# RWKV attention and a mixture of experts on one core: experts' hidden split ahead of the next rows, slot buffers doubled, V differences on VectorE, new order in the last project round, at the seam and in the first output batch

## The reference, cut to what matters

```python
# attention (RWKV): a token's mix with the token before it, four projections, a scan, one projection out
xx = prev - x;  xk, xv, xr, xg = (x + xx * tm for tm in (tm_k, tm_v, tm_r, tm_g))
r, k, v, g = xr @ Wr.T, xk @ Wk.T, xv @ Wv.T, sigmoid(xg @ Wg.T)
# scan over t, e = exp(k_t): out = (a + exp(u) e v) / (b + exp(u) e);  a = w a + e v;  b = w b + e
attn = layernorm((sigmoid(r) * wkv * g) @ Wo.T) * ln_g + ln_b
# experts: rms norm, 32 experts, each token takes its 4 best, at most 256 tokens an expert
probs = softmax(z @ w_router);  w_topk, sel = top_k(probs, 4)
y[e] = (silu(buf[e] @ w_gate[e]) * (buf[e] @ w_up[e])) @ w_down[e]        # 512 -> 352 -> 512
shared = sigmoid(z @ w_shared_gate) * ((silu(z @ sw_gate) * (z @ sw_up)) @ sw_down)   # 512 -> 1408 -> 512
```

## Time and profile before

| | us |
|---|---|
| median of 3 runs (1730.23 to 1732.56) | 1730.6 |
| the profiled execution, own time | 1733.92 |
| its span, first to last instruction | 1732.0 |
| first expert's first product | 448.35 |
| first product of the output stage | 898.23 |
| PE idle in the engine's rows | 4% |

### The profile page before, as it was taken

One profiled execution on the slowest core, in us unless ns is written; L12 is line 12 of the kernel. 1 busy time (PEld: TensorE's weight loads), 2 busy tenths in 40 slices (PEclk: granted clock), 3 DMA queues, 4 the chain that ended last, 5 costly groups with the idle time before them and its releaser, 6 DMA issues.

```text
span 1732.0 us, 26222 instructions
## 1 busy us (share of the span) xinstructions
PE 1661.9 (96%) x8496; PEld 1403.0 (81%) x8496; DVE 1280.8 (74%) x1868; ACT 695.3 (40%) x1189; POOL 879.4 (51%) x733
## 2 busy tenths in 40 slices
PE   5899999999799999999998899999999999999998
PEld 4677877777799999999986678888788888888887
DVE  7999999996455555555559877786777768687776
ACT  4565655554466666666653312121121212112121
POOL 3888888877444444444436635242443524253251
PEclk9999999999999999999999999999999999999999
DMA  4444433434566666666676655465445334433431
GB/s 158 164 171 171 151 141 135 157 122 173 186 223 223 231 229 230 231 229 234 227 263 207 213 192 183 141 207 170 158 149 167 117 137 142 138 118 110 164 104 43
DMA packets 122938, 299.17 MB, mean 173 GB/s; under 512 B 20508, under 2 KB 31772, under 8 KB 118240
## 3 DMA queue, kind: packets, MB, share of 16 engines
q1 hardware_dynamic: 103104, 263.82, 43.2%
q0 software_dynamic: 19456, 33.67, 6.9%
q10 hardware_dynamic: 288, 0.52, 0.1%
HBM read 233.34 MB, written 81.36 MB: 182 GB/s over the span
## 4 chain that ended last, share of the span: by engine, by line
PE 65%; DVE 14%; issue 11%; POOL 5%; ACT 2%; DMA 2%; DVEq 0%; POOLq 0%; SPq 0%; ACTq 0%
PE bank L1923 24%; PE bank L1298 16%; PE bank L1937 12%; PE bank L1954 5%; PE bank L1325 3%; POOL slot_tokens L370 3%; DVE mixf L683 3%; DVE e_xT L1237 2%; PE bank L947 2%; PE bank L1290 2%; POOL mix L356 1%; ACT e_xT L1158 1%; DVE seen L735 1%; DVE valid L750 1%; DVE e_h L1248 1%
## 5 line engine op out<-in xcount | busy, mean ns | idle before, releaser
L947 PE MATMUL bank<-mix,w 128*128 128x512 f32 x1536 | 367.5, 398 | 19.9 <-DVE sr L704 8.0
L947 PEld LDWEIGHTS bank<-mix,w 128*128 128x128 f32 x1536 | 290.4, 191 | 87.1 <-POOL mix L356 8.9
L1923 PE MATMUL bank<-s_zT,s_wu 128*128 128x512 f32 x1056 | 259.9, 396 | 12.1 <-DVE s_act_g L1732 11.2
L1923 PE MATMUL bank<-s_zT,s_wg 128*128 128x512 f32 x1056 | 254.3, 390 | 0.9 <-ACT s_act_g L1643 0.5
L1937 PE MATMUL bank<-s_wd,s_h 128*128 128x512 f32 x1056 | 254.7, 390 | 0.0
L1923 PEld LDWEIGHTS bank<-s_zT,s_wu 128*128 128x128 f32 x1056 | 200.8, 191 | 57.3 <-issue 15.5
L1923 PEld LDWEIGHTS bank<-s_zT,s_wg 128*128 128x128 f32 x1056 | 197.8, 188 | 43.8 <-issue 2.2
L1937 PEld LDWEIGHTS bank<-s_wd,s_h 128*128 128x128 f32 x1056 | 199.2, 189 | 42.1 <-DVE s_h L1738 0.3
L1118 POOL TENSOR_TENSOR e_wg<-e_g_in,e_wg 128x1408 fp32r<-128x1408 f32 x31 | 100.4, 3239 | 225.6 <-ACT e_wg L1142 225.6
L1555 POOL DMA_INDIRECT s_picked<-y_rows,s_slot x128 | 140.3, 1096 | 84.9 <-DVE s_total L1788 45.2
L1654 ACT ACTIVATE s_h<-s_act_g 128x512 fp32r<-128x512 f32 x88 | 55.6, 632 | 292.3 <-DVE s_act_g L1732 289.1
(11 more groups left out here) (158 smaller groups left out, 2455.2 us busy)
## 6 DMA issues: line engine op xcount, KB each, us to landing
s_wu<-wu_split SPq DMA_DIRECT2D x77, 512.0 KB
e_g_in<-in_w_gate SPq DMA_DIRECT2D x32, 704.0 KB
e_u_in<-in_w_up SPq DMA_DIRECT2D x32, 704.0 KB
e_d_in<-in_w_down SPq DMA_DIRECT2D x32, 512.0 KB
y_rows<-e_y SPq DMA_DIRECT2D x32, 512.0 KB, 2.9
s_zT<-zT_parts SPq DMA_DIRECT2D x16, 1024.0 KB, 7.3
zT_parts<-zT_hi SPq DMA_DIRECT2D x8, 1024.0 KB
zT_parts<-zT_lo SPq DMA_DIRECT2D x8, 1024.0 KB
```

The lines of the kernel that those rows point to most:

```text
L947: last = pe.matmul(pj[m][:], w[i][:, w_part, k, m * P:(m + 1) * P], mix[:, i % 2, k, x_part, :], start=(k == 0 and q == 0), stop=(k == KC ...
L1923: last = pe.matmul(into[:], w[:, w_part, k, :], zT[:, x_part, k, :], start=(q == 0 and k == 0), stop=(q == 2 and k == KC - 1))
```

## The change

It changes orders and buffers; what is computed is the same.

- **Project rounds.** V's differences move from GpSimd to VectorE (`mix_lo(b, V_)`). `make_gate(b, 0..1)` moves from behind `make_zT` into it, behind its first two products; on ScalarE `gate_g(b, 0..1)` goes ahead of the four `z_hi`. The slot numbers and the scatter semaphore are doubled by half. Running counts become one scan (`counted`, `fresh`, `seen`). The copies into `keep` go to ScalarE (`make_z`, `keep_route`). `count` moves one pair of R later, `assign(0)` from the first round into round 1. The scatters are spread anew: 6 of batch b behind its own round's G, 10 in the next; GpSimd runs none in the first round and 22 in round 1.
- **Last round.** `score(LAST)` moves from inside round 6 to the head of the last round, turn_score and count into K's pairs; all differences are VectorE's; on SP store_ekv goes ahead of expert 0's weights, the table read goes ahead of expert 1's, and expert 1's up and down weights wait for the gather of expert 0. ScalarE puts `first_gate_up` behind all mixes and ahead of gate_r.
- **Experts.** hidden_hi(2) goes ahead of rows_hi, hidden_lo(2) ahead of rows_lo.
- **Output stage.** `hidden` writes into the PSUM banks `ob` for tiles 0 to 9. For batch 0, four gate pieces are loaded ahead and split during the last expert, D pieces run three ahead, and the base rows, the first scan, `current` and `inverse` of batch 0 move into or behind the last expert. keep_y(31) on ScalarE stands behind them. The gathers of batch 0 move into its step 0, since `ahead` lies on the tile `picked`.

```diff
 # project, VectorE one_round
+            gates(b - 1, 2)
+            if second:
+                assign(0, 0, 0)
             for k in range(KC):
                 make_mix(b, half, V_, k)
+            for k in range(KC):
+                mix_lo(b, V_, k)
 ...
-            for k in range(KC):
-                make_mix(b + 1, 1 - half, K_, k)
-            if not tail:
-                make_zT(b + 1, 1 - half)
-            make_gate(b, 0)
-            make_gate(b, 1)
+            for k in range(KC):
+                make_mix(b + 1, 1 - half, K_, k)
+            make_zT(b + 1, 1 - half, lambda: gates(b, 0))
 # project, GpSimd one_round
-            mix_lo(b, V_)
+            scatter(b - 1, 1 - half, at, at + KC)
             norm_scales(b + 1, 1 - half)
-            mix_lo_among(b, R_, b - 1, MORE)
-            scatter(b - 1, MORE + KC, NT * TOPK)
-            mix_lo(b, G_)
-            scatter(b, 0, SOME)
-            mix_lo_among(b + 1, K_, b, SOME)
-            scatter(b, SOME + KC, MORE)
+            mix_lo_among(b, R_, b - 1, 1 - half, at + KC, last)
+            if second:
+                scatter(b - 1, 1 - half, at + 2 * KC, last - KC)
+                at = last - 3 * KC
+            mix_lo_among(b, G_, b - 1, 1 - half, at + 2 * KC, last)
+            scatter(b, half, 0, MORE - KC)
+            mix_lo_among(b + 1, K_, b, half, MORE - KC, MORE)
 # assign
-            wait(dve, scattered, b * NT * TOPK * 16)
+            wait(dve, scattered[half], uses * NT * TOPK * 16)
+            wait(dve, route_kept, b)
 # SP last_round
             store_gate(LAST - 1)
+            store_zT(LAST)
             store_ek(LAST)
+            store_ekv(LAST)
             first_weights()
-            store_ekv(LAST)
+            read_table()
             second_weights()
 # ScalarE last_round
+            for k in range(KC):
+                mix_hi(LAST, G_, k)
             first_gate_up()
-            for k in range(KC):
-                mix_hi(LAST, G_, k)
-            first_down()
+            keep_route(LAST, FIRST_HALF)
             for m in range(KC):
                 gate_r(LAST, m)
+            first_down()
 # TensorE last_round
+            score(LAST)
+            project(LAST, K_, 0, {2: lambda: turn_score(LAST)})
+            project(LAST, K_, 1, {3: lambda: count(LAST)})
 # experts, ScalarE (VectorE alike)
             silu(e, 2)
+            hidden_hi(e, 2)
             if more:
                 rows_hi(e + 1, 1 - half)
-            hidden_hi(e, 2)
 # output stage
+    def hidden_at(f, i):
+        return ob[f % 2][:] if f < NFS - 1 else act_g[:, i, :]
-            dve.tensor_tensor(act_g[:, i, :], act_g[:, i, :], up[:], ALU.mult).then_inc(h_made, 1)
+            dve.tensor_tensor(hidden_at(f, i), act_g[:, i, :], up[:], ALU.mult).then_inc(h_made, 1)
 # output stage, batch 0, VectorE: in the last expert, last_third and last_fourth behind hidden_lo(2)
+        def last_third():
+            gate_lo(2)
+            dve.wait_ge(setup, 3)
+            sums(0, 0, 0)
+
+        def last_fourth():
+            gate_lo(3)
+            gate_lo(4)
+            current(0, 0)
+            inverse(0, 0)
 # ScalarE, behind hidden_hi(2) of the last expert and ahead of its keep_y
+        def last_fourth():
+            weight_hi(U, 1)
+            weight_hi(D, 1)
+            for j in range(NT):
+                make_base(0, j)
 # GpSimd, ahead of batch 0
+            weight_lo(D, 2)
+            pool.wait_ge(piece_lo[G], AHEAD + 1)
             pool.memset(picked[:], 0.0).then_inc(setup, 1)
+            pool.wait_ge(c_loaded, 32)
+            for j in range(NT):
+                add_base(0, j)
 # GpSimd, step 0 of batch 0
+                if zero(b) and f == 0:
+                    gather(0, 0)
+                    gather(0, 1)
```

381 lines of the change are left out of this document (198 added, 183 removed).

## The result

| | before | after |
|---|---|---|
| median of the runs, us | 1730.4 (1729.2 to 1732.6) | 1709.7 (1708.8 to 1710.5) |
| ratio | | 0.9874, interval 0.9860 to 0.9888 |
| profiled execution, us | 1733.9 | 1710.3 |
| its span, us | 1732.0 | 1708.3 |

What follows compares the result with a forecast made beforehand. TensorE, busy 96%, was taken as the bound, with gains only where it waits or runs at its lower clock. Rounds 8.3, seam 10.2, experts 15.5 and output batch 0 12.7 sum to 46.7, giving 1684 us, range 1668 to 1708.

Steps and rivals of the forecast that it cites:

- 4.70 against 4.13: Experts: gate products to down take 4.70, the last expert 4.13; 0.5 taken per expert, 15.5 us in all.
- rival (e): Experts: rows_lo comes after TensorE wants it, 31 us per further us of delay, 1750 with 3.2 us; chance 0.03.
- 48.5 apart: Project rounds: waits for sr L704 gone and K's starts 48.5 us apart; three passages at 1.6 give 4.8 us.
- rival (c): Project rounds: the wait changes its name from sr to zT_lo or xn, part 1 becomes 0, 1693; chance 0.07.
- 3.5 forecast: Batch 1's round: 54 to 55 us instead of 56.07, plus earlier start and clock; gain 3.5, between 0 and 8.
- 5.7 for 10.2: Last round and seam: 115.0 us from batch 6's K to first expert product becomes 104.8; gain 10.2, between 6 and 15.
- slot numbers at about 17: Last round: slot numbers made about 17 us after the end of batch 6's G, with a score wait of about 1.1.
- Rival (a): Seam: weights late, G waits for gate_r behind first_gate_up; takes back the 10.2, 1694; chance 0.09.
- 2.1 for 12.7: Output batch 0: of 21.2 us lost, 8.5 stay lost; gain 12.7, between 3 and 16.
- The delay of hidden(0), priced at 1.3: Output batch 0: VectorE reaches hidden(0) at about 906.5 to 907 instead of 904.66, 1.3 us late.
- That of make_att(0), priced at 1: Output batch 0: make_att(0) waits for GpSimd behind four base sums and four gathers, 1 us.
- Rival (b): Output batch 0: VectorE stays the bound, hidden(0) late and make_att waiting; 12.7 becomes 1, 1696; chance 0.09.

Runs made afterwards that it cites:

- e1: Kernel before the change, with only the experts' edit (third hidden tile's split ahead of the next expert's rows on ScalarE and VectorE): 1716.5 us, ratio 0.9908.
- e7: Changed kernel with the third and fourth sigmoid of R ahead of the high parts of the next K mixes on ScalarE: 1711.0 us.
- e6: e7 with count(b) on TensorE ahead of R's first pair instead of between R's pairs: 1704.6 us.
- e12: e6 with round 1 re-queued: assign(0) behind V mixes, differences and row statistics, route copy behind make_xn, norm_scales ahead of the first four scatters: 1706.1 us.
- e15: e6 with POOL's round 1 scatters spread: four among the next K's differences, batch 1's six behind those: 1707.8 us.
- e17: Changed kernel with the edits of rounds, output stage and seam summed, plus round 1's four G differences on VectorE in place of POOL: 1693.3 us.
- e9: Changed kernel with 8 of the last batch's 16 scatters left out (result not the reference's): 1709.0 us.
- e2: Changed kernel with the output stage's hidden tile back in act_g (SBUF) for all tiles: 1708.4 us.
- e3: Changed kernel with POOL's first gated_sum moved into the last expert, ahead of the base sums and four gathers: 1711.2 us.
- e4: Changed kernel with gate piece 5 loaded in the last expert and Wo's loads behind the other pieces of f = 0: 1709.1 us.
- e11: Changed kernel with the output stage's start re-queued on three engines and second staging tiles for the first batch's U and D pieces: 1701.0 us.
- e10: Changed kernel without three reciprocals of the first output batch, 10 us less VectorE work (result not the reference's): 1704.4 us.
- e14: e6 and e11 together, the sum of the edits of the rounds and the output stage on the changed kernel: 1698.2 us.

## Why the prediction was wrong, step by step

**Experts: right.** 14.9 for 15.5. The step that read the cost from the last expert (4.70 against 4.13) and not from the profile's 0.20 held, and e1 shows that nothing else has a part in it. rows_lo was in time: rival (e), the slower side, did not come.

**Middle rounds: mechanism right, half the size.** The wait for sr L704 went in all of them. What failed is "48.5 apart": they came 49.2 to 49.4 apart. The new order costs 0.7 to 1.0 in each, and the round from batch 2 to 3, which had no such wait before, became 1.1 longer. The step that failed is a term that the prediction put at nothing by leaving it out: that `count(b)` moves one pair of R later, and that VectorE waits for it. VectorE stands 1.2 us for it in the changed kernel and up to 2.5 in e7, the K mixes behind. From e7 to e6 only count moves back, and the three rounds from 3 on lose 0.4 to 0.9 each; rival (c) had a wait that changes its name, but named zT_lo or xn. The differences that VectorE makes of the mixes, V's among them, were not held by GpSimd: all 40 took 0.68 to 0.73 us.

**Rounds 0 and 1: 3.5 forecast, 0.4 measured.** The terms in the prediction give 2.6 to 3.6, so 3.5 was already their good end. Round 0 gained 4.0 and round 1 lost 3.6. I had listed the right things (assign(0) ahead, 22 scatters, differences late by 2.7 and 1.1) but summed delays of single instructions. Against that speak e12 and e15, in which moving assign(0) and spreading the scatters won nothing over the two rounds, and e17, in which 5.2 us less work on POOL gave 4.4: the term that was missing is POOL's sum of work.

**Seam: 5.7 for 10.2.** 0.8 of the missing 4.5 is the round before it. In the other 3.7 the term "slot numbers at about 17" fails: the first scatter starts 22.4 us behind 381.84. 1.4 is a wait of the score of 2.48 and not 1.1, 1.6 the score at the lower clock, 1.8 a stop of VectorE ahead of assign, which three of the other twelve executions with this last round have and nine don't. Scatters (24.7 for 25.5), table and gather (8.9 for 9.1) and the first product (3.9 for 4.6) were close. Rival (a) was there, 2.87 us at G, and the prediction called it hidden, by 3.6 us (48 under 51.6). It was, but by 1.6 us only, and in eight of the thirteen executions the rows were there first or at most 0.4 us late; e9 shows that it is the next limit.

**First output batch: 2.1 for 12.7, nearly half of the miss.** And the 2.1 are not from the edits of the output stage: e1, without them, took 104.6, and the waits rose from 11.9 to 13.7. That this stretch gained at all against the kernel before is luck: the granted clock there was 0.94, and 0.97 in both others, and no run shows why. The forecast took one cause, VectorE held by POOL in instructions with two SBUF inputs, and let it go with the hidden tile's new place. Every difference from a bank did take 0.69, as forecast, but e2 shows that this is worth about 1 us in the new order. The delay of hidden(0), priced at 1.3, did not come: it starts 6.46 us into the stage, 6.43 before. That of make_att(0), priced at 1, came as an idle stretch of 4.92 us on VectorE, and one of 4.80 for the late gate piece had no term at all. By e3 and e4 neither costs much alone. The ring of load, high part, difference and next load wasn't in the prediction at all, though ScalarE's waits for landings show it (19.1 us in that stretch before the change, 30.0 after it); e11 takes 4.3 us out with it. Rival (b) gave 1 for this part, near the 2.1, but for a reason that e10 shows to be only a part: 10 us off VectorE gave 3.9.

So the sum failed by three of its four parts, all on the same side. Where a step put several moved things together, it counted what the change removes in full and what it adds as hidden.

## What to carry to other kernels

A wait that goes is worth only the distance to the next chain that ends there; work out that chain from its own rows before taking the whole wait as a gain, and where two end close together, move both. Before counting a gain of a stretch, look at what the same stretch takes in a kernel that doesn't edit it: here the first output batch had won more without its edits than with them. For each moved instruction write down who waits for it, also when the instruction is as small as count. In a stage that loads, splits and multiplies piece by piece, look at the waits of the splitting engine for landings: 38.8 us there is a ring that wants a second staging tile, whatever the matmul's own waits name.

## What the runs showed of the hardware

VectorE stops with no releaser at the same place of every execution, at the second turn of the output stage's loop: 4.47 us in the kernel before, 4.61 after, between 4.1 and 7.6 in the others. In four kernels (e9, e10, e14, e15) it was 6 or more, and there the output batch in which it falls, from one project_out to the next, took 103.6 to 106.3 us in place of 101.8 to 103.1. Only e1 had 104.7 with a stop of 4.63, so this is not the one cause. From the sum of the edits:

```profile
1199.11 0.69 DVE L1799 TENSOR_TENSOR s_h<-bank,s_h 128x512 fp32r<-128x512 f32 x1 [6.04 <-issue]
```

The same kind of stop ahead of assign at the seam was 1.81 us in the changed kernel, 3.23 in e3, 1.64 in e4, 1.72 in e7, and absent in the nine others with the changed kernel's last round. Their cause was not tried.

The granted clock differs too where the work does not: 0.94 in the first output batch of the kernel before and 0.97 in e1, with the same output stage, waits of 11.9 and 11.6 us, and 108.1 against 104.6 us. So one profile can't settle an edit of 2 us by its total, and by a stretch only where kernels that leave it alone agree.
